# A three-stage decoder layer on one core: attention without its unread products and with values copied first, and a second expert layer with routing logits on column tiles

## What is computed

```python
x = x + attn(layernorm(x), ...)            # 8 heads, low-rank q and kv, 64 sequences of 64 tokens
x = x + xattn(layernorm(x), ctx, ...)      # 8 experts, top 2 chosen from the context's logits
x = x + ffn(layernorm(x), ...)             # 32 experts, top 8 within the best 4 of 8 groups, and a shared one

# the router of the last one
scores = sigmoid(h @ gate_w.T); sc = scores + gate_bias
group_scores = top_k(sc.reshape(-1, 8, 4), 2)[0].sum(-1)      # the best 4 groups stay
combine = one_hot(top 8 of the masked sc) * scores, normed to sum 2.5
g = silu(h @ w_gate.T); u = h @ w_up.T
out = sum over experts of (g * u * combine) @ w_down.T + shared
```

## Time and profile before

| | us |
|---|---|
| median of 3 runs | 756.46 |
| lowest and highest run | 754.01, 759.85 |
| the profiled execution: device time | 756.52 |
| the profiled execution: span of the trace | 754.8 |
| PE busy | 669.3 (89%) |
| DVE busy | 552.5 (73%) |
| ACT busy | 353.1 (47%) |
| POOL busy | 345.7 (46%) |

### The profile page before, as it was taken

The page is one execution under the profiler, slowest core; times in us unless marked ns, Lnnn a source line. Parts: engine busy times, 40 slices in busy tenths (PEclk is TensorE's granted clock), DMA queues, the critical chain, the costliest instruction groups (busy, mean ns, idle before and its releaser), DMA issues.

```text
span 754.8 us, 11001 instructions
## 1 busy us (share of the span) xinstructions
PE 669.3 (89%) x3456; PEld 475.5 (63%) x3456; DVE 552.5 (73%) x1318; ACT 353.1 (47%) x628; POOL 345.7 (46%) x386
## 2 busy tenths in 40 slices
PE   6868999999708999999992988999999999999997
PEld 5535666666506777777771755666666666666664
DVE  4367877779517999999964786777868695958564
ACT  3844666655204666666663533444343424353221
POOL 5111377778867999999957324040312213000000
PEclk9967999999958999999997898999999999999999
DMA  9900300000023466666311293354555545444442
GB/s 227 366 11 0 92 30 29 29 29 34 38 77 88 127 206 193 179 188 193 113 56 45 59 207 87 90 154 109 132 112 138 129 112 132 111 130 112 124 116 58
DMA packets 73816, 84.14 MB, mean 111 GB/s; under 512 B 15057, under 2 KB 42683, under 8 KB 73758
## 3 DMA queue, kind: packets, MB, share of 16 engines
q1 hardware_dynamic: 68536, 74.93, 36.4%
q0 software_dynamic: 4096, 8.40, 3.8%
q10 hardware_dynamic: 1126, 0.11, 0.1%
HBM read 64.48 MB, written 18.87 MB: 110 GB/s over the span
## 4 chain that ended last, share of the span: by engine, by line
PE 57%; POOL 18%; DVE 11%; issue 7%; ACT 4%; DMA 2%; another core or an unknown queue 0%; SPq 0%; POOLq 0%; ACTq 0%; DVEq 0%
PE pair_banks L1625 15%; POOL h1h L586 7%; PE bank L1408 7%; PE bank L1410 6%; PE bank L1409 6%; POOL W2l L571 4%; PE pair_banks L1315 4%; PE score_banks L1410 3%; PE score_banks L1408 3%; PE score_banks L1409 3%; POOL W2h L566 3%; PE bank L1447 2%; PE pair_banks L1493 2%; POOL x_sorted L544 2%; PE bank L1467 2%
## 5 line engine op out<-in xcount | busy, mean ns | idle before, releaser
L865 ACT ACTIVATE r_s<-bank 128x512 f32<-128x512 f32 x136 | 81.1, 598 | 160.7 <-PE bank L1410 150.8
L1625 PE MATMUL pair_banks<-t_s,Dn 128*128 128x512 f32 x272 | 138.6, 595 | 0.0
L1150 DVE TENSOR_TENSOR h1l<-r,h1h 128x512 fp32r<-128x512 f32 x92 | 113.4, 1251 | 16.2 <-POOL h1h L586 16.2
L1408 PE MATMUL bank<-fxh,Gh 128*128 128x512 f32 x136 | 97.6, 718 | 0.0
L1265 DVE TENSOR_TENSOR rc_s<-r_s,score_banks 128x512 f32<-128x512 f32 x90 | 61.5, 684 | 49.0 <-ACT r_s L865 39.5
L1278 DVE TENSOR_TENSOR t_s<-rc_s,bcb 128x512 f32<-128x512 f32 x128 | 87.4, 685 | 4.1 <-DMA bcb<-c_rows 2.6
L586 POOL TENSOR_SCALAR h1h<-r 128x512 fp32r<-128x512 f32 x92 | 73.8, 806 | 19.6 <-ACT r L816 17.3
L605 POOL TENSOR_TENSOR mvp<-mvp,meps 128x4 f32<-128x4 f32 x8 | 1.6, 197 | 172.4 <-DVE mvp L1188 172.4
L544 POOL DMA_INDIRECT x_sorted<-xsb,posi x64 | 64.2, 1003 | 31.9 <-DVE xsb L1077 19.8
L597 POOL DMA_INDIRECT yg<-y_sorted,posi x64 | 64.3, 1005 | 25.3 <-issue 18.4
L1625 PEld LDWEIGHTS pair_banks<-t_s,Dn 128*128 128x128 f32 x272 | 51.4, 190 | 14.7 <-issue 3.8
(11 more groups left out here) (286 smaller groups left out, 1611.4 us busy)
## 6 DMA issues: line engine op xcount, KB each, us to landing
bcb<-c_rows SPq DMA_DIRECT2D x128, 256.0 KB
wraw<-in_L_xattn_W SPq DMA_DIRECT2D x46, 256.0 KB, 2.9
x_sorted<-wraw SPq DMA_DIRECT2D x1, 5888.0 KB, 17.4
xg<-x_sorted SPq DMA_DIRECT2D x23, 256.0 KB, 3.4
y_sorted<-ysb SPq DMA_DIRECT2D x23, 256.0 KB, 3.0
ctxb<-in_ctx SPq DMA_DIRECT2D x8, 256.0 KB, 6.0
out<-x_all SPq DMA_DIRECT2D x8, 256.0 KB
x_all<-in_x SPq DMA_DIRECT2D x2, 512.0 KB, 5.2
```

What stands on the lines that cost most here:

```text
L865: act.activation(r_s[:, n % RB2, :], bank[n % 3][:, :], ACT.Silu).then_inc(F["act"], 1)
L1150: tt(h1l[:, n % NB1, :], r1[:, n % RB1, :], h1h[:, n % NB1, :].bitcast(F32), ALU.subtract)\
L1408: mm(dst, wh, xh, start=start, stop=False)
L1625: mm(bank[6][:, :], Dn[:, weights_of(p), :], t_s[:, n % TB2, :], start=(p == 0), stop=(p == NC2 - 1))\
```

## The change

In attention:
- the three unread products of `output` go; in their place 54 products into the same columns run after the last slot, nine behind each of the last six slots' scatters;
- ACT copies `uS` (`values`) ahead of `ph` and of the exponential, in each step;
- `xl` is made in the step of `xh`, one step earlier, behind `maximum`; `add_out_bias` one step earlier too;
- the last three slots are normalised on DVE instead of POOL;
- the first router's work on DVE is spread over steps 1 to 8, its weights come after step 33, and `ranks` one step later.

In the first expert layer the biases share the weights' semaphores. In the second:
- logits are computed with `gwT` as the stationary operand, four tiles of 32 columns that land on 32 partitions each; ACT copies them out (`lgS`), and one transpose brings them back (`back`);
- the combine weights are transposed in one piece, `cT` is 128x128, and four transfers of 16 KB store it instead of one of 64 KB;
- sigmoid and routing stand one step later; for block 1 all from the logits on stands one to two steps later.

```diff
-HEAD = dict(..., xh=((-6, 0),), xl=((-5, 0),), kv=((-5, 0),),
+HEAD = dict(..., xh=((-6, 0),), xl=((-6, 0),), kv=((-5, 0),),
+NV = NT - 3
-SLOTS = dict(..., fxl=3, lg=4, sc=5, rt_a=6, rt_b=7,
-             rt_c=8, rt_d=9, c_ps=14, cT=14, accS=8, tp=10, x2=12)
-FIRST = dict(cmbB=4, paggr=4, pnb=5, pxn=7, pxT_ps=9, pxT=9, fxl=10, lg=11, sc=11, rt_a=11, rt_b=12, rt_c=13, rt_d=14,
-             c_ps=16, cT=16)
+SLOTS = dict(..., fxl=3, lg=4, lgS=4, back=5, sc=6, rt_a=7,
+             rt_b=8, rt_c=9, rt_d=10, c_ps=14, cT=14, accS=8, tp=10, x2=12)
+FIRST = dict(cmbB=4, paggr=4, pnb=5, pxn=7, pxT_ps=9, pxT=9, fxl=10, lg=12, lgS=12, back=13, sc=13, rt_a=13, rt_b=14, rt_c=15,
+             rt_d=16, c_ps=18, cT=18)
...
-                sp.dma_start(bcur[:, b % BB, :].unsqueeze(1), bT[:, ds(e, 1), :]).then_inc(s_b[b % BB], 16)
+                sp.dma_start(bcur[:, b % BB, :].unsqueeze(1), bT[:, ds(e, 1), :]).then_inc(s_w[b % WB], 16)
...
-                sp.dma_start(cs[j], cT[:, :]).then_inc(s_cs, 16)
-                sp.wait_ge(s_cs, 16 * (j + 1))
+                for t in range(TPS):
+                    sp.dma_start(cs[j][:, t * P:(t + 1) * P], cT[t * E2:(t + 1) * E2, :]).then_inc(s_cs, 16)
+                sp.wait_ge(s_cs, 16 * TPS * (j + 1))
...
-                if 0 <= m < NT:
+                if 0 <= m < NV:
                     normalise_p(m)
...
+                if 0 <= n - LAG["u"] < NT:
+                    values(n - LAG["u"])
                 if 0 <= n - LAG["pT"] < NT:
                     transposed_p(n - LAG["pT"])
                 if 0 <= n - LAG["exp"] < NT:
                     exponent(n - LAG["exp"])
...
-                if 0 <= n - LAG["u"] < NT:
-                    values(n - LAG["u"])
...
+            def prep_lg(j):
+                act.wait_ge(F["lg"], j + 1)
+                copy(lgS[:, :], bank[7][:, 0:P]).then_inc(F["lgS"], 1)
...
+                if n == 3:
+                    router1_picked()
                     out_bias()
-                    router1_counts()
-                if n == 4:
+                if n == 5:
                     router1_bases()
-                if n == 5:
+                if n == 6:
                     router1_positions()
-                if n == 6:
+                if n == 8:
+                    router1_blocks()
+                if n == NT + 2:
                     router1_weights()
-                if n == 7:
-                    router1_blocks()
...
+                    if u >= NV:
+                        dve.wait_ge(A["rden"], u + 1)
+                        at = sm[:, u % NP, :].rearrange("p (h t) -> p h t", h=H)
+                        tt(at, at, rden[:, u % NP, :, :].to_broadcast([P, H, S]), ALU.mult).then_inc(A["pv"], 1)
...
-                for c in range(3):
-                    mm(bank[0][:, (c + 1) * D:(c + 2) * D], tri[:, :], onesM[:, :], start=True, stop=True)
...
+            pe.wait_ge(A["x1"], NT)
+            for m in range(NT - 6, NT):
+                pe.wait_ge(s_sc[m % SC], 32 * (m // SC + 1))
+                for c in range(9):
+                    mm(bank[0][:, c % 3 * D:(c % 3 + 1) * D], tri[:, :], onesM[:, :], start=True, stop=True)
...
-                    ins = mm(bank[7][:, t * E2:(t + 1) * E2], xTt[:, t * P:(t + 1) * P], gwT[:, :],
+                    ins = mm(bank[7][t * E2:(t + 1) * E2, 0:P], gwT[:, :], xTt[:, t * P:(t + 1) * P],
                              start=True, stop=True)
...
+            def prep_back(j):
+                pe.wait_ge(F["lgS"], j + 1)
+                transpose(bank[7][:, P:2 * P], lgS[:, :]).then_inc(F["back"], 1)
...
-                for t in range(TPS):
-                    ins = transpose(bank[7][0:E2, t * P:(t + 1) * P], cw[:, t, :])
-                ins.then_inc(F["c_ps"], 1)
+                transpose(bank[7][:, 0:P], cw[:, :, :].rearrange("p t e -> p (t e)")).then_inc(F["c_ps"], 1)
```

More of the change, by code:

```diff
@@ L82 @@
 NBG = NP2 // BG
-SLOTS = dict(cmbA=-5, cmbB=-4, paggr=-3, prstd=-2, pnb=-1, pxn=0, pxT_ps=2, pxT=2, fxl=3, lg=4, sc=5, rt_a=6, rt_b=7,
-             rt_c=8, rt_d=9, c_ps=14, cT=14, accS=8, tp=10, x2=12)
-FIRST = dict(cmbB=4, paggr=4, pnb=5, pxn=7, pxT_ps=9, pxT=9, fxl=10, lg=11, sc=11, rt_a=11, rt_b=12, rt_c=13, rt_d=14,
-             c_ps=16, cT=16)
+SLOTS = dict(cmbA=-5, cmbB=-4, paggr=-3, prstd=-2, pnb=-1, pxn=0, pxT_ps=2, pxT=2, fxl=3, lg=4, lgS=4, back=5, sc=6, rt_a=7,
+             rt_b=8, rt_c=9, rt_d=10, c_ps=14, cT=14, accS=8, tp=10, x2=12)
+FIRST = dict(cmbB=4, paggr=4, pnb=5, pxn=7, pxT_ps=9, pxT=9, fxl=10, lg=12, lgS=12, back=13, sc=13, rt_a=13, rt_b=14, rt_c=15,
+             rt_d=16, c_ps=18, cT=18)
 def steps_at(i, p):
-    steps = [(name, 1) for name, s in FIRST.items() if i == 0 and s == p]
+    steps = [(name, 1) for name, s in FIRST.items() if divmod(s, NC2) == (i, p)]
     return steps + [(name, j) for name, s in SLOTS.items() if name not in ("accS", "tp", "x2")
@@ L264, in decoder_kernel @@
             fxh, fxl = (a(n, [P, 2 * ST], F32R) for n in ("fxh", "fxl"))
-            cT = a("cT", [E2, ST])
+            cT = a("cT", [P, P])
+            lgS = a("lgS", [P, P])
             cw = a("cw", [P, TPS, E2])
@@ L299, in decoder_kernel @@
         s_w = [sem(f"expert_in{i}") for i in range(WB)]
-        s_b = [sem(f"expert_bias_in{i}") for i in range(BB)]
         s_xg = [sem(f"sorted_in{i}") for i in range(XB)]
@@ L323, in decoder_kernel @@
         F = {n: sem("f2_" + n) for n in (
-            "up gate act rc t dn accS tp x2 cmb1 cmb bst pstat prstd pnb pxn pxT_ps fxh xT fxl lg sc cw c_ps cT "
+            "up gate act rc t dn accS tp x2 cmb1 cmb bst pstat prstd pnb pxn pxT_ps fxh xT fxl lg lgS back sc cw c_ps cT "
             "chain").split()}
@@ L832, in prep_x @@
                 copy(xTt[:, :], bank[7][:, :]).then_inc(F["xT"], 1)
+            def prep_lg(j):
+                act.wait_ge(F["lg"], j + 1)
+                copy(lgS[:, :], bank[7][:, 0:P]).then_inc(F["lgS"], 1)
             def prep_sc(j):
-                act.wait_ge(F["lg"], j + 1)
-                act.activation(scores[:, :, :], bank[7][:, 0:TPS * E2].rearrange("p (t e) -> p t e", t=TPS),
+                act.wait_ge(F["back"], j + 1)
+                act.activation(scores[:, :, :], bank[7][:, P:P + TPS * E2].rearrange("p (t e) -> p t e", t=TPS),
                                ACT.Sigmoid).then_inc(F["sc"], 1)
@@ L841, in prep_c @@
                 if j >= 1:
-                    act.wait_ge(s_cs, 16 * j)
-                copy(cT[:, :], bank[7][0:E2, :]).then_inc(F["cT"], 1)
+                    act.wait_ge(s_cs, 16 * TPS * j)
+                copy(cT[:, :], bank[7][:, 0:P]).then_inc(F["cT"], 1)
             def acc_out(j):
@@ L858, in _ @@
             prep_x(0)
+            prep_lg(0)
             prep_sc(0)
@@ L879, in _ @@
                             prep_x(j)
+                        if name == "lgS":
+                            prep_lg(j)
                         if name == "sc":
@@ L1102, in _ @@
                 o, u, m = n - LAG["out"], n - LAG["sum"], n - LAG["xs"]
+                if n == 5:
+                    router1_counts()
                 if 0 <= o < NT:
                     residual1(o)
-                for step in head_steps(n, ("xl", "kvlo")):
-                    head(*step)
+                if n == 0:
+                    head("kvlo", 1, 0)
+                for name, j, part in head_steps(n, ("kvlo",)):
+                    if j != 1:
+                        head(name, j, part)
                 if 0 <= u < NT:
@@ L1125, in _ @@
                     maximum(n)
+                for step in head_steps(n, ("xl",)):
+                    head(*step)
                 statistics_rest(n)
                 router1(n)
-                if n % TPS == 1 and 5 <= n < NT + 5:
-                    add_out_bias((n - 5) // TPS)
+                if n % TPS == 0 and 4 <= n < NT + 4:
+                    add_out_bias((n - 4) // TPS)
             def sorted_low(b):
@@ L1470, in transposed_p @@
             def transposed_p(n):
-                pe.wait_ge(A["p"], n + 1)
+                if n < NV:
+                    pe.wait_ge(A["p"], n + 1)
+                else:
+                    pe.wait_ge(A["pv"], n - NV + 1)
                 if n == 0:
@@ L1676, in _ @@
                             prep_logits(j)
+                        if name == "back":
+                            prep_back(j)
                         if name == "c_ps":
```

27 lines of the change are left out of this document (17 added, 10 removed).

## The result

The changed kernel takes 734.2 us, median of 4 runs (731.8 to 737.7), against 755.2 of the kernel before on the same chip (4 runs, 753.5 to 759.9). The ratio is 0.9709, with a 95% interval of 0.9675 to 0.9742: by the medians 21.0 us less, where 29.6 were forecast. The time lies inside the range of 713 to 742.

A forecast was written before the change was run, and what follows sets the result against it. PE was taken to set the pace in attention's full stretch and the second expert layer, POOL in the first. Terms 5.0 + 9.5 + 3.0 + 1.1 + 4.2 + 7.1 - 0.3 = 29.6 us off 756.46 gave 727 us, range 713 to 742.

The forecast's parts named there:

- Steps 1 to 9: First steps of attention: earlier `xl` (3.1 us), spread router work and removed products together gain 5.0 us, between 3 and 8.
- 22 slots: Attention's full stretch: without the unread products the pace falls from 4.53 to 4.1 us a slot, gaining 9.5 us (3 to 16).
- A floor for each engine with its own gaps: Attention's 22 slots: floors of about 3.6 us a slot for PE, 3.8 for DVE, 3.7 for POOL; pace above the largest.
- The low clock in parts: Rival, chance 0.15: in attention, two to eight slots run at 1.2 GHz without the unread products; total 731 to 743 us.
- The stated limit of 0.95: Sign for attention's full stretch: the forecast is wrong if the clock there is below 0.95.
- POOL's tail: End of attention: three normalisations of 1.06 us leave POOL, which runs there without a wait; gain 3.0 us, at least 2.2.
- The 54 products: Behind attention's last slots: first block's transposes and products start at full clock; gain 1.1 us, loss of 2 if it is low.
- Block 0 and block 1: Second layer's preparation: block 1 gains 7.1 us by shorter waits and no low clock; block 0's four store issues cost 0.3.
- Blocks 2 to 7: Second expert layer: shorter logits and transposes save 0.7 us of PE a block, 4.2 us in six (2.5 to 5.5).
- a tile switch of 0.29 us at either end: Rival, chance 0.04: the second layer's 32-column logits drain PE before and after, costing 3.5 of the 4.2 us; total 730.4.
- DVE and POOL in each other's way: Rival, chance 0.12: the engines slow each other reading SBUF in attention; pace 4.4 us a slot, 6.6 us less gained, 733.5.

The follow-up runs named there:

- first_early: Changed kernel with block 1's preparation in the second expert layer put back as near its old places as the new steps allow: 738.8 us, ratio 0.9762.
- pool_short_norm: Changed kernel with POOL's normalisation cut to one of the eight heads, leaving out part of the computation: 731.8 us, ratio 0.9687.
- pool_norm_all: Changed kernel with the last three normalisations given back from DVE to POOL: 736.5 us, ratio 0.9769.
- xl_late: Changed kernel with `xl` back one step, ahead of the sums, and the second group's low half of `kvS` back in step 1: 740.5 us, ratio 0.9817.
- one_store: Changed kernel with `cw` laid out expert first, so one 64 KB transfer stores `cT` instead of four of 16 KB: 735.6 us, ratio 0.9722.
- attention_alone: Changed kernel with the second expert layer of the kernel before (old logits, four transposes, one store, old places): 744.8 us, ratio 0.9856.
- products_back: Changed kernel with the three unread products a slot put back ahead of the output product: 744.9 us, ratio 0.9877.
- act_old_order: Changed kernel with `values` on ACT moved back behind the transposed probabilities and the exponential: 747.3 us, ratio 0.9915.

## Why the prediction came out as it did

The total was right within its range, by terms that missed on both sides. The last scatter was forecast at 203 and came at 203.6, but that is luck: the first steps gained 3.9 us more than forecast and the 22 slots 3.7 less.

*Steps 1 to 9: 5.0 forecast, 8.9 measured.* What was said of `xl` was right: 3.1 us forecast, 3.2 measured (the row "to `xl`" of the table above, 4.46 against 1.28); 1.4 of it the router's spreading gives by itself. Removed products and router were to bring the other 1.9. What failed is a term put at nothing: the earlier `kvS` of the second group, 3.0 us, isn't in the sum at all. Of the rest, 0.5 us is the router's piece between the maxima of steps 1 and 2, 1.5 had already been gained by the maximum of step 0, and 0.7 came behind `xl`. That 1.5 can't be trusted: the kernels with the changed attention lie between 35.0 and 37.1 us there. The clock was full from 59.7 on instead of from 73.0, but that isn't needed for the gain: in `first_early` and `pool_short_norm` it was low again from 80.5 to 87.4 and from 76.9 to 87.1, and their first scatters come at 80.7 and 78.9.

*22 slots: 9.5 forecast, 5.8 measured.* The step that failed is that one pace was taken for all of them. 4.53 us is the mean of two kinds of slots. Where every fourth has a head part they took 4.76 us and take 4.31, 0.44 less. Where none has one they took 4.0 us at POOL's own pace, and still do (four slots in 16.0 us before and after, and 12.7 in `pool_short_norm`), so nothing could be gained in them. By parts: the first four slots gained 1.6 us, the next twelve 5.3, and the last six lost 1.1. The forecast had both numbers, 4.53 and 4.0, and set 4.1 near the second because it took POOL's bare length for what would hold every slot; in the slots with head parts `pool_short_norm` shows that POOL only follows. A floor for each engine with its own gaps (3.6, 3.8, 3.7) doesn't show a ring between PE and DVE, and that the 0.43 us a slot forecast and the 0.44 measured there agree is luck: 0.43 was the distance from the mean of all slots to POOL's pace.

The gain was also put down to the products alone, and ACT's new order only kept their cover from being missed. The order brings 0.28 us a slot with the products still there, more than the 0.19 that taking them out adds. What the text said of the old order, that the cover would be missed, held: the products' removal alone makes the kernel slower.

*The low clock in parts*, the first rival, came too, at its low end: one stretch with slots of 4.92 and 5.29 us, which take 4.22 and 3.78 in `pool_norm_all`, where the clock was full there: 2.2 us. The second low stretch fell on slots that POOL holds and cost nothing. The stated limit of 0.95 was just met.

*POOL's tail: 3.0 forecast, 2.8 measured*, and 2.5 in `pool_norm_all`.

*The 54 products: 1.1 forecast, 0.6 measured at the first `h1h`* (17.4 gained at the last scatter, 18.0 there) *and nothing at the last one* (17.0). Full clock at the transposes was foreseen rightly, and whether it would hold through PE's next wait, 1.41 us for `xl` of the first block, was not asked.

*Block 0 and block 1: 6.8 forecast together, 3.1 measured* (17.3 gained at the first transposes of block 0's preparation, 412.40 to 395.11, and 20.4 at the logits of block 2). The four issues took 1.72 us, close to the 1.5 forecast, but the first `t_s` waits 4.11 us instead of 2.56: that is 1.5 us, and PE idles 1.53 at the product behind it, where it did not before. The forecast had 0.6 and counted half of it, without naming what hides the other half. In block 1 the wait at `cw` fell as forecast (2.33, forecast 1.5), but the low clock behind it came anyway, 3.2 us of it, where the forecast had hoped for none. That was not certain either: in `xl_late` a wait of 2.46 us at the same place, and in `one_store` one of 2.95, were followed by full clock. A 0.75 us wait for `fxl` in block 2 is new. The 3.1 is one execution against another: from the first logits of the layer to those of block 2 the traces lie 1.3 us apart in the changed layer and 2.9 in the old one.

*Blocks 2 to 7: 4.2 forecast, 2.9 measured*, 3.2 in `attention_alone`, 0.5 us a block instead of 0.7. Logits take 0.42 us (0.33 forecast), `cw` 0.30, back 0.27: 0.97 + 0.60 - 0.42 - 0.30 - 0.27 = 0.58 a block, 3.5 in six; the forms were priced by their own length, and what they add between their neighbours is less. From the start of the down product ahead of the logits to that of the full-width product behind them it is 1.31 us (489.90 to 491.21) instead of 1.67 (510.64 to 512.31): 0.36 saved with both switches in it, where a tile switch of 0.29 us at either end, a rival, would have left 0.06.

*DVE and POOL in each other's way*, a rival, doesn't show in the changed kernel's pace (13.71 against 13.70 us of DVE in four slots), but does in `products_back` and `act_old_order`.

## What to carry over

Work that nobody reads can be the cover of another engine's copy. Before it is taken out, look at what the next instruction waits for: here the order on ACT had to change first, and the products alone cost 1.4%. Split a stage into its kinds of step before you take a mean: here 4.53 us was 4.76 with a head part and 4.0 without, and only the first could be shortened. Where no engine is full, find the ring of waits; work taken off an engine that only follows there gives nothing. And read the whole diff into the sum: a move of one operation by one step, left out of the list, was worth 3.0 us, as much as the move that was priced.

## What the runs showed of the hardware

- A DVE addition of 128x512 with both inputs in SBUF took 0.68 us, and 1.87 when a POOL multiplication of 1.05 us began inside it. In all 13 such pairs of the kernel before, `products_back` and `act_old_order` it ended 0.56 us after the multiplication did, whichever began first: in `products_back` it began at 114.02, the multiplication at 114.28, they ended at 115.89 and 115.33; in the kernel before 110.01 and 109.65, 111.26 and 110.70. POOL's operation was not longer for it. The Trainium skill's "GPSIMD Engine Reference", Specifications, has the two share an interface. The trace agrees with the rule for the multiplication, and shows no price for a scatter: the addition at 128.47 in the changed kernel took 0.68 beside one of POOL (128.34, 0.97 us).
- After a wait of 2.02 us of PE at 147.46 the clock was at 1.2 GHz from 148.4 to 155.2, though PE was busy 14.5 of 17.2 us in the slots before. After 2.04 us at 116.93 in `products_back` the same from 117.9. The length of one wait doesn't decide it: the wait of 2.94 us for `kvS` at 78.35 in the changed kernel left the clock full, and the same wait of 2.94 at 79.5 in `first_early`, the same code, was followed by 1.2 GHz from 80.5 to 87.4. By the last scatter these two executions are 3.4 us apart.
- Runs of one kernel differ by the clock they are granted. The ten of `act_old_order` lie between 0.939 with a span of 752.2 us and 0.966 with 743.5: about 3 us for each hundredth.
- Four DMA issues of 16 KB in place of one took 1.72 us on SP's queue, 0.32 for the first and 0.42 for each of the others, against 0.32 for the one.
